# Moving the feed-forward tail of a query tile from the end of the next tile's step into the middle of its head loop (sandwich layer, eight cores)

## The reference

```python
# attention, on h = layernorm(x)
Q, K, V = h @ wq, h @ wk, h @ wv              # 16 heads of 64
local = window_attention(Q, K, V)             # each query sees 256 keys back
GQ = h @ wgq; GK, GV = pool32(h @ wgk), pool32(h @ wgv)
rem = softmax(GQ GK^T / 8, causal by chunk) GV @ r_out_w
out = sigmoid(Q.gl) * local + sigmoid(Q.gr) * rem
x1  = x + layernorm(out @ w_out)
# feed-forward, on u = layernorm(x1)
u_dq = clip(round(u * 127/max|u|), -128, 127) * max|u|/127
x2   = x1 + layernorm(u_dq @ ternary_w.T * scale + bias)
```

## Time and profile before

| | us |
|---|---|
| median of the runs | 3415.43 |
| runs | 3414.04 to 3416.82 |
| the profiled execution, its own time | 3422.15 |
| span of its slowest core, from first to last instruction | 3420.4 |
| spans of the 8 cores | 3404.4 to 3420.4 |

### The profile page before, as it was taken

The page is one execution under the profiler, slowest core; times in us unless marked ns, Lnnn a source line. Parts: engine busy times, 40 slices in busy tenths (PEclk is TensorE's granted clock), DMA queues, the critical chain, the costliest instruction groups (busy, mean ns, idle before and its releaser), DMA issues.

```text
span 3420.4 us, 37834 instructions; the slowest of 8 cores (3404.4 to 3420.4 us)
## 1 busy us (share of the span) xinstructions
PE 2836.0 (83%) x10608; PEld 2012.3 (59%) x10624; DVE 751.0 (22%) x1614; ACT 499.4 (15%) x1337; POOL 19.9 (1%) x36
## 2 busy tenths in 40 slices
PE   0269888898889979899889988899798997889994
PEld 0146756566755748467565667557484675656672
DVE  0210231123300333104311133013231043111333
ACT  0111111111100111112111111011111021111121
POOL 0000000000000000000000000000000000000000
PEclk9999566985579665895668855786658956698566
DMA  3334002220032100330022300321003300222000
GB/s 88 92 96 136 17 1 79 75 89 1 7 116 87 41 7 25 92 111 16 7 79 68 93 3 7 116 74 53 7 22 94 111 16 7 73 74 74 1 7 13
DMA packets 72539, 185.78 MB, mean 54 GB/s; under 512 B 12960, under 2 KB 15520, under 8 KB 72352
## 3 DMA queue, kind: packets, MB, share of 16 engines
q1 hardware_dynamic: 70048, 174.98, 17.0%
q10 hardware_dynamic: 2304, 8.39, 0.6%
HBM read 173.90 MB, written 8.39 MB: 53 GB/s over the span
## 4 chain that ended last, share of the span: by engine, by line
PE 77%; issue 7%; DMA 7%; DVE 5%; ACT 4%; DVEq 0%; SPq 0%; ACTq 0%; POOL 0%; POOLq 0%
PE pp L390 13%; PE pp L507 12%; PE pp L655 8%; PE pp L488 7%; PE pp L513 7%; PE pp L430 6%; PE pp L361 4%; PE pp L613 4%; PE pp L450 3%; PE pp L784 2%; PE pp L461 2%; PE pp L372 2%; PE pp L327 1%; DMA ringg<-wgv 1%; PE pp L768 1%
## 5 line engine op out<-in xcount | busy, mean ns | idle before, releaser
L507 PE MATMUL pp<-vb,PTs 128*128 128x64 f32 x1536 | 514.5, 439 | 82.4 <-ACT PTs L499 82.4
L390 PE MATMUL pp<-hfm,ringw 128*128 128x256 f32 x2048 | 465.3, 391 | 33.5 <-DMA ringw<-wq 24.1
L507 PEld LDWEIGHTS pp<-vb,PTs 128*128 128x128 f32 x1536 | 413.2, 329 | 107.3 <-issue 107.3
L390 PEld LDWEIGHTS pp<-hfm,ringw 128*128 128x128 f32 x2048 | 402.6, 197 | 96.8 <-issue 38.9
L513 PEld LDWEIGHTS pp<-cvec_s,PTs 128*128 128x128 f32 x1536 | 419.6, 333 | 0.0
L513 PE MATMUL pp<-cvec_s,PTs 128*128 128x1 f32 x1536 | 408.6, 335 | 0.0
L488 PE MATMUL pp<-qfm,kb 64*128 64x128 f32 x1536 | 312.1, 463 | 19.0
L655 PE MATMUL pp<-wouts,mixfm 128*128 128x512 f32 x512 | 263.1, 679 | 12.0 <-ACT mixfm L647 12.0
L499 ACT ACTIVATE PTs<-pp,cvec_s 128x384 f32<-128x384 f32 x256 | 169.8, 670 | 705.1 <-PE pp L513 639.3
L488 PEld LDWEIGHTS pp<-qfm,kb 64*128 64x128 f32 x1536 | 216.0, 293 | 91.1 <-issue 88.9
L430 PE MATMUL pp<-ringw,hfm 128*128 128x512 f32 x512 | 221.6, 593 | 7.1 <-ACT kb L415 7.1
(11 more groups left out here) (122 smaller groups left out, 1760.2 us busy)
## 6 DMA issues: line engine op xcount, KB each, us to landing
ringw<-wq SPq DMA_DIRECT2D x64, 512.0 KB, 4.2
ringw<-wk SPq DMA_DIRECT2D x64, 512.0 KB, 3.6
ringw<-wv SPq DMA_DIRECT2D x64, 512.0 KB, 3.6
ringg<-wgk SPq DMA_DIRECT2D x64, 256.0 KB, 2.7
ringg<-wgv SPq DMA_DIRECT2D x64, 256.0 KB, 2.7
ringg<-wgq SPq DMA_DIRECT2D x64, 256.0 KB, 3.0
xr<-x SPq DMA_DIRECT2D x16, 512.0 KB, 4.1
y<-mixfm ACTq DMA_DIRECT2D x16, 512.0 KB, 2.7
```

The lines of the kernel that those rows point to most:

```text
L390: P("pe", lambda E, i=i, k=k, m=m, bk=bk, reg=reg: E.matmul(psum[bk][:, reg:reg + 256], ring_w[i][:, 128 * m:128 * (m + 1)], h_fm[k][:, 0: ...
L507: P("pe", lambda E, h=h, s_=s_, slot=slot, lbank=lbank: E.matmul(psum[lbank][:, (h % 8) * 64:(h % 8) * 64 + 64], PTs[h % 2][:, 128 * s_:12 ...
```

## The change

The part of tile g-1 that follows its 40 small operations (`epi_ktffn`, `epi_yffn`, `epi_ln4`, `epi_y2`) moves from `be_mix`, the place behind it and the place behind `be_wout` into the head loop of tile g, between head pairs 3 and 4. For that the 40 small operations are drained 8 at a time over pairs 0 to 3, with the last 8 straight after pair 3, and no longer 5 at a time over all 8 pairs. The transposes of the burst use bank 2, so the softmax sums of the heads, which are open at that place, move to columns 384 to 399 of bank 0, behind the 384 columns of scores of the even pairs. Their key is then `ps0`.

```diff
                     P("pe", lambda E, h=h, s_=s_: E.matmul(
-                        psum[2][:, h:h + 1], PTs[h % 2][:, 128 * s_:128 * (s_ + 1)],
+                        psum[0][:, 384 + h:385 + h], PTs[h % 2][:, 128 * s_:128 * (s_ + 1)],
                         c1, start=(s_ == 0), stop=(s_ == 2)),
-                      reads=(f"PTs{h%2}", "cvec"), writes=("ps2",), dbg="Psum mm")
+                      reads=(f"PTs{h%2}", "cvec"), writes=("ps0",), dbg="Psum mm")
...
-                P("act", lambda E: E.copy(sm[:, 40:56], psum[2][:, 0:16]),
-                  reads=("ps2",), writes=("smsums",), dbg="smsums evac")
+                P("act", lambda E: E.copy(sm[:, 40:56], psum[0][:, 384:400]),
+                  reads=("ps0",), writes=("smsums",), dbg="smsums evac")
...
-            dr5 = lambda: drain(5)
+            dr8 = lambda: drain(8)
             for g in range(NQT):
                 if g + 2 < NQT:
                     fe_A_ln(g + 2)
-                be_heads(g, list(range(0, 4)), after_pair=dr5)
-                be_heads(g, list(range(4, 8)), after_pair=dr5)
+                be_heads(g, list(range(0, 4)), after_pair=dr8)
+                drain(10**9)
+                if g >= 1:
+                    epi_ktffn(g - 1)
+                    epi_yffn(g - 1)
+                    epi_ln4(g - 1)
+                    epi_y2(g - 1)
+                be_heads(g, list(range(4, 8)))
                 if g == 0:
                     dma_load("maskv", maskv[:], m1_h[:, :])
-                drain(10**9)
                 if g + 2 < NQT:
                     fe_A_hT(g + 2)
 
                 def fill(g=g):
                     if g % 2 == 1 and g + 2 < NQT:
                         fe_Qpair(g + 1)
-                    if g >= 1:
-                        epi_ktffn(g - 1)
-                ycb = (lambda gg=g - 1: epi_yffn(gg)) if g >= 1 else None
-                be_mix(g, ktffn_cb=fill, yffn_cb=ycb)
-                if g >= 1:
-                    epi_ln4(g - 1)
+                be_mix(g, ktffn_cb=fill)
                 be_wout(g)
-                if g >= 1:
-                    epi_y2(g - 1)
                 epi_evac(g)
```

## The result

| | before | changed |
|---|---|---|
| median of the runs, us | 3420.93 (18 runs) | 3439.93 (19 runs) |
| ratio to before, 95% interval | | 1.0042 (1.0024 to 1.0061) |
| span of the slowest core (core 2), profiled execution | 3420.4 | 3432.7 |
| mean span of the 8 cores | 3411.6 | 3416.3 |

The change makes the kernel slightly slower: 0.42%, which is 14 us of 3421, with 8 to 21 us as the interval. I had forecast 45.3 us. The sign and the "within 2%" were right and the size was three times too large.

The account below looks back on a forecast made before the run. PE, busy for 83% of the span, was taken as the bound. Even tiles +51.8, odd +18.9, tile 15 +6.6 and stores -32.0 gave +45.3 us, a median of 3461 from 3415.4; 8-in-10 range 3418 to 3494.

Parts of the forecast that it names:

- The burst in its new place: Heads, between pairs 3 and 4: the chain of small operations makes the burst add 12.0 us in tiles 1 to 15.
- rival D: Burst costs no more than in its old place, 10.0 us, clock neutral: +8.2 us, so 3424; chance 0.18.
- What the mix gains: be_mix without the burst: 5.0 us less in even tiles and tile 15, 8.5 and 0.4 less in odd tiles.
- The clock: L587 to L601 lose the high clock: +1.8 us even tiles, +1.0 others; scores of pair 4 gain it: -1.1.
- the cap: Heads: V products of pair 4 can't start before 9.4 us after the burst, so only 1.1 us is gained.
- rival B: Burst raises PE's clock and busy heads keep it high: 50 to 166 us gained, middle 3352; chance 0.07.
- The shared bank: Heads: scores of even pairs wait for the last sum in bank 0, three times a tile; +0.2 us.
- the slack of 1.2 us: Heads behind the burst: PE's own 10.6 us of work against 9.4 us until pair 4's exponential is ready.
- rival C: Added waits in the heads bite: 2.5 us per tile, 37 us added, 3498; chance 0.17.
- The store: ACT no longer waits for the store: -4.0 us for each of tiles 3, 5 to 15 and the run's end, -32.0.
- Small terms: The w_out product's 0.68 us wait for ACT copies goes, -0.5 us a tile; bank waits of even-pair scores add +0.2.

Follow-up runs that it names:

- e5: Changed kernel with sums in bank 2, burst transposes in banks 0 and 1, and the burst issued ahead of the statistics; ratio to before 0.9925.
- e7: Kernel before with only the softmax sums moved to bank 0; ratio to before 1.0011.
- e4: Changed kernel with the softmax sums back in bank 2 and the burst's transposes in banks 0 and 1; ratio to before 1.0155.
- e12: Changed kernel with only epi_y2 back behind be_wout, second run on another chip; ratio to before 1.0095.
- e10: Kernel before with epi_yffn, epi_ln4 and epi_y2 all in the mix, burst in its old place, second run on another chip; ratio to before 0.9802.
- e11: Kernel before with only epi_ln4 moved to right behind epi_yffn in the mix, second run on another chip; ratio to before 0.9935.
- e9: Changed kernel with four extra ACT squares ahead of the copies for the w_out product; ratio to before 1.0197.

## Why the prediction was right in its sign and wrong in its size

**The burst in its new place: right.** 12.2 us between the pairs in tile 2 and 11.6 in the mean, 12.0 forecast, along the chain I had read from the end of the run; rival D's 10.0 falls. e5 shows that the chain is the cause: off it, 9.5 us are left. D's total of 3424, +8.2 us, is nearer to the measured 14 than mine, but by chance: it had the burst at 10.0 and the clock neutral, and neither holds.

**What the mix gains: right.** Even tiles' heads, L555, wait and burst together changed by +42.2 us, +42.7 forecast.

**The clock: right in its terms, with one surplus that is taken back.** L587 to L601 lost 23.5 us, 20.6 forecast. The scores of pair 4 ran high (1.82 us where I had 1.6). The V products of pair 3 did too, which I had not priced; it brings nothing more, since PE then waits 2.4 us for the exponential of pair 4. That is the cap I had put at 9.4 us behind the burst (9.6 measured), so that 10.6 - 9.6 = 1.0 us is gained where I had 1.1. For rival B the periods behind it had to stay high; the granted clock says they do not. Stretches of the changed kernel:

```profile
787.00:793.00 6.00, 5.81 (x44) 5.02 (x43) 4.57 (x10) 1.55 (x3) 0.00 (x0) 0.94 0.00 0
793.00:799.00 6.00, 3.59 (x19) 3.32 (x17) 2.87 (x5) 1.83 (x3) 0.00 (x0) 0.50 0.22 89
```

A mean of 0.94 in 787 to 793 is 0.7 us at 0.50, so the clock falls at about 792.3, 6 us behind the burst and ahead of the wait, while PE is busy (5.81 of 6 us) with V products and scores. The pairs behind run at 0.50. The Trainium skill, page "TensorE: Matmul & The Clock Gate", section "What's actually happening", says that the throttle is set by how busy PE has been recently. Read as PE's busy time, that is against this row, as it was against the 54 us at 0.50 in the earlier trace rows, and B's time does not come.

**The shared bank and the slack: rival C falls.** e7 and e4 put the bank at about half a microsecond a tile (0.2 forecast), and the slack of 1.2 us behind the burst did not bite beyond what the quicker V products left open. The DVE operations of the chain take the same time in the trace of before, in the loop, as at its end with PE idle: L826 1.22 us, L822 0.81, L722 0.48 in either place.

**The store: right in its mechanism, a little small.** 4.0 us forecast, 4.9 measured for a tile that follows an even one. The wait of L507 fell from 9.39 to 4.53 us. My 4.05 ran from the start of L826 to L666. But without the store L666 does not start where the product ends; it starts when the product's first bank is done, 0.7 us before that (872.52 against 873.24), where it had started 4.2 us behind (870.41 against 866.25). In e12 the odd heads grow by 22.5 us when the term is put back, and in e10 they shrink by 33.4 against e11.

**The step that failed: "Small terms".** "The w_out product waits 0.68 us for ACT copies that stand behind L818; they don't now: -0.5." The operation was the right one and its price was four times too small. On core 2 the 16 products are 31.2 us cheaper, 2.0 each: 0.75 of wait and 1.2 of the product itself, because with PE's wait ahead of L655 the clock stays low for longer. With L638 the stage is 36.2 us shorter in the mean of the cores, where I had 7.5; that is 29 of the 37 us that the forecast is off. I had read the wait from the earlier trace rows and stopped there. The 16.52 us of the product stood in the same row. It was to be seen that part of it ran at the low level, and I priced that for L587, L596 and L601 but never asked it of L655. e11 takes the norm alone and gets the 31 us on core 2 (30 in the mean); e9 brings the wait back and most of the length with it.

The other 8 us are the store term (6.5), 0.3 us a tile in the rest of the odd heads and burst (2), L613 and the projections (1.5) and 1 in the even heads and behind tile 15, less 3 that L587 to L601 lost beyond the forecast.

Put together, by the stage sums, the change is two improvements of 26 us (norm: e11 against before) and 39 us (store: e10 against e11), and a burst moved out of its cover at 73 us (changed against e10): +8. The parts hold for this order of steps; e12 shows that they don't simply add up in another. e10 leaves the burst where it was and takes both improvements: 2% faster than before.

## What to carry to other kernels

When a change moves several things, run each alone: here the part that was meant as a side effect carried the gain, and the moved work, which had stood in another chain's shadow, cost more than both gains. Price a short wait ahead of a long PE product not by its own length alone; look whether the product's first passes run at the low clock and how far into it the clock rises. And on an engine with a fixed order, look at what stands right ahead of the copies that PE waits for.

## What the runs showed of the hardware that I had not expected

- A wait of 0.7 us (up to 1.5) ahead of the w_out product went with a rise of the clock 5.2 us into it instead of 2.5, and with 1.3 us more of length; four ACT operations of a microsecond each were enough to bring most of it back (e9). In the mean of 120 products 5.1 us of each are at 0.50 before, 2.6 after and 4.7 in e9.
- The float32 V products follow the clock when it is high: 12 scores in 1.82 us and 3.31 us for the V products and sums of a pair, 5.14 at the low level. They do not hold it: it falls some 6 us behind the burst with PE busy for 5.81 of 6 us.
- An accumulation that shares a bank with the scores of other pairs cost about 0.5 us a tile in the stage sums and nothing that a ratio of 1.0011 (0.9986 to 1.0037) can tell.
